# Graph layers of one batch up front instead of two, and each later batch's graph layers four steps ahead of the attention

## What is computed

```
adj = layernorm(x)                        # 256 x 256, used as a soft adjacency
h   = ctx
for W, a_self, a_neigh, b in (layer 0, layer 1):          # two graph attention layers, 8 heads of 32
    feat  = h @ W                                         # per head
    e     = leaky_relu(feat.a_self (rows) + feat.a_neigh (columns), 0.2) - 1e10 * (1 - adj)
    h     = elu(softmax(e) @ feat + b)                    # heads side by side: 256 x 256
x1  = x + h
y   = layernorm(x1)
r   = y + attention(rmsnorm(y))           # 16 query heads, 4 key heads, causal, rotary, q/k rmsnorm
out = x1 + r + mixture(rmsnorm(r))        # 8 experts, the two best of each row, silu(gate) * up, down
```

## Time and profile before

| | |
|---|---|
| median of three runs | 656.95 us |
| profiled execution | 656.72 us, span 654.9 us |
| PE busy | 607.1 us, 93% of the span |
| DVE, POOL, ACT busy | 435.1, 306.8, 269.0 us (66, 47, 41%) |
| mean granted TensorE clock | 0.979 |

### The profile page before, as it was taken

How to read it: one execution, slowest core, us unless ns; L and a number is a source line. 1 busy time by engine, 2 the same in 40 slices (tenths; PEclk the granted TensorE clock), 3 DMA queues, 4 the chain that set the end, 5 groups by cost and what they waited for, 6 DMA issues and landing times.

```text
span 654.9 us, 10357 instructions
## 1 busy us (share of the span) xinstructions
PE 607.1 (93%) x3269; PEld 435.6 (67%) x3269; DVE 435.1 (66%) x1279; ACT 269.0 (41%) x653; POOL 306.8 (47%) x588
## 2 busy tenths in 40 slices
PE   3799899789799999989699999989999998999998
PEld 2278468336677798736587788736668873666886
DVE  4897688598755587599756487466644646664463
ACT  2363454164665342164665342045740204574020
POOL 1493486478844240378854150378630038763000
PEclk9999899889899999999899999989999998999999
DMA  8920000000000000000000000000000000000000
GB/s 285 385 72 3 1 2 1 16 5 2 1 1 2 1 2 17 16 2 1 1 2 1 1 2 0 18 0 2 1 1 1 2 17 1 2 0 2 1 2 16
DMA packets 8729, 14.41 MB, mean 22 GB/s; under 512 B 908, under 2 KB 7372, under 8 KB 8420
## 3 DMA queue, kind: packets, MB, share of 16 engines
q1 hardware_dynamic: 8676, 13.76, 5.9%
HBM read 12.70 MB, written 1.05 MB: 21 GB/s over the span
## 4 chain that ended last, share of the span: by engine, by line
PE 65%; DVE 19%; issue 5%; POOL 5%; ACT 4%; DMA 1%; DVEq 0%; POOLq 0%; SPq 0%; ACTq 0%
PE bank L616 14%; PE bank L514 10%; PE bank L574 5%; PE ob L488 5%; PE bank L638 5%; PE bank L593 4%; PE bank L560 3%; PE tb L477 3%; DVE ssq L1024 2%; PE bank L589 2%; PE bank L585 2%; ACT prob L727 2%; DVE tt L959 2%; DVE m L1021 2%; PE zb L469 2%
## 5 line engine op out<-in xcount | busy, mean ns | idle before, releaser
L560 PE MATMUL bank<-wqkv_sb,hT 128*128 128x512 f32 x192 | 92.8, 623 | 0.8 <-ACT v_sb L703 0.8
L727 ACT ACTIVATE prob<-bank,sneg,rms 128x128 f32<-128x128 f32 (+1 forms) x128 | 64.0, 508 | 58.6 <-DVE sneg L1053 58.4
L837 POOL TENSOR_TENSOR m<-early,rope_s 128x256 f32<-128x256 f32 x80 | 73.1, 938 | 31.4 <-ACT early L708 30.9
L514 PE MATMUL bank<-m,wgu_sb 128*128 128x128 f32 (+1 forms) x480 | 85.6, 329 | 0.7 <-DVE early L1100 0.6
L795 POOL TENSOR_SCALAR tt<-tt,gmn 128x256 f32<-128x256 f32 x96 | 66.9, 706 | 36.2 <-DVE gmn L959 35.8
L514 PEld LDWEIGHTS bank<-m,wgu_sb 128*128 128x128 f32 x480 | 70.9, 191 | 8.9 <-DVE early L1100 2.1
L853 POOL TENSOR_SCALAR prob<-prob,srcp 128x128 f32<-128x128 f32 (+1 forms) x128 | 53.4, 435 | 48.2 <-DVE srcp L1124 48.0
L574 PE MATMUL bank<-kT,qT 128*128 128x128 f32 (+1 forms) x256 | 60.9, 354 | 1.8 <-ACT prob L727 1.8
L616 PE MATMUL bank<-wo_sb,qT 128*128 128x256 f32 x256 | 59.0, 382 | 0.7 <-ACT qT L733 0.7
L560 PEld LDWEIGHTS bank<-wqkv_sb,hT 128*128 128x128 f32 x192 | 35.4, 196 | 36.3 <-issue 33.0
L708 ACT ACTIVATE early<-bank 128x512 f32<-128x512 f32 x40 | 24.1, 602 | 79.5 <-PE bank L560 77.2
(11 more groups left out here) (200 smaller groups left out, 1182.3 us busy)
## 6 DMA issues: line engine op xcount, KB each, us to landing
wqkv_sb<-wqkv_dram SPq DMA_DIRECT2D x1, 3072.0 KB, 12.2
wgu_sb<-wgu_dram SPq DMA_DIRECT2D x2, 1408.0 KB, 10.8
wo_sb<-wo_dram SPq DMA_DIRECT2D x1, 2048.0 KB, 17.6
wd_sb<-wd_dram SPq DMA_DIRECT2D x1, 1408.0 KB, 14.7
out_dram<-rows SPq DMA_DIRECT2D x8, 128.0 KB, 1.7
xin<-x_dram SPq DMA_DIRECT2D x3, 256.0 KB, 2.7
rows<-gat_rows_dram SPq DMA_DIRECT2D x2, 256.0 KB, 2.9
kT<-x_dram SPq DMA_DIRECT2D x1, 256.0 KB, 3.8
```

Source lines behind the costliest of these rows:

```text
L514: mm = pe.matmul(ps[:, m * N + c0:m * N + c1], wgu_sb[:, m, k, n * P:(n + 1) * P], tokT[:, k, c0:c1], start=(k == 0), stop=(k == KT - 1))
L560: mm = pe.matmul(ps[:, :], hT[:, k, t * P:(t + 1) * P], wqkv_sb[:, k, c * G * HD:(c + 1) * G * HD], start=(k == 0), stop=(k == KT - 1))
L727: ins = act.activation(prob[:, n % 5, i * nk:(i + 1) * nk], ps[:, i * nk:(i + 1) * nk], ACT.Exp, bias=sneg[:, n, i:i + 1], scale=rq(g, t, ...
L837: ins = pool.tensor_tensor(dst[:, :, c, :], src[:, :, 1 - c, :], s_, ALU.mult)
```

## The change

`PLAN` has the graph layers of batch 0 alone up front. Those of batch 1 run beside the tail of batch 0, those of 2 beside the tail of 1, those of 3 beside the tail of 2; only the last pass has none. In the passes graph layers and prep stand four steps ahead of the tail: steps 4 to 43 of a pass have the steps 8 to 47 of the next batch's two strands (in the passes after the first the steps 0 to 43 have 4 to 47), and the last four steps have the steps 0 to 3 of the batch after that. Batch 1 has no earlier pass, so the steps 0 to 3 of the first pass have two of its steps each.

With it: one set of buffers, banks and semaphores for the graph layers; two `x1` buffers instead of three; the inputs of batch 1 are loaded behind the weights, those of batch `b + 2` ahead of the stores of batch `b`; the Newton steps of batch 0's layer norm are made by DVE (nine instructions) and not by POOL (twelve); `WAKE` has other places and 127 products; setup work of layer 1 is one step earlier.

```diff
-SET, SEQ, XS = (0, 1, 0, 0), (0, 0, 1, 2), 3
-BEHIND = 2
+SEQ, XS = (0, 1, 2, 3), 2
-TERMS1_AT, ROPE_AT = (15, 16), (25, 26, 27)
-WAKE = {2: 3, 7: 4, 8: 14, 19: 3, 20: 3, 21: 3, 22: 3, 23: 3, 24: 3, 25: 3, 26: 3, 27: 3, 28: 3, 30: 4, 31: 14, 43: 10, 45: 8}
-WAKE.update({s: 2 for s in tuple(range(9, 19)) + tuple(range(32, 43))})
+TERMS1_AT, ROPE_AT = (14, 15), (25, 26, 27)
+WAKE = {1: 2, 2: 4, 5: 2, 6: 2, 7: 2, 8: 14, 18: 5, 20: 3, 22: 3, 24: 6, 28: 3, 29: 3, 30: 3, 31: 12, 41: 18, 43: 6, 45: 3}
+WAKE.update({s: 2 for s in tuple(range(9, 18)) + tuple(range(32, 41))})
+AHEAD = 4
 PLAN = []
 for step in range(STEPS):
-    PLAN += [("gat", 0, step), ("prep", 0, step + PREP_LEAD), ("gat", 1, step - BEHIND)]
+    PLAN += [("gat", 0, step), ("prep", 0, step + PREP_LEAD)]
 for batch in range(B):
     for step in range(STEPS):
-        PLAN += [("gat", batch + 2, step)] if batch + 2 < B else []
-        PLAN += [("prep", batch + 1, step)] if batch + 1 < B else []
+        if batch == 0 and step < AHEAD:
+            PLAN += [("gat", 1, 2 * step), ("gat", 1, 2 * step + 1)]
+        elif batch + 1 < B and step + AHEAD < STEPS:
+            PLAN += [("gat", batch + 1, step + AHEAD), ("prep", batch + 1, step + AHEAD)]
+        elif batch + 2 < B:
+            PLAN += [("gat", batch + 2, step + AHEAD - STEPS)]
         PLAN += [("tail", batch, step)]
...
-            for b in range(2, B):
-                load_inputs(b)
+            load_inputs(1)
             for b in range(B):
+                if b + 2 < B:
+                    load_inputs(b + 2)
                 store(b)
...
-                    if b == 1:
-                        keep_clock(WAKE.get(s + BEHIND, 0))
+                    if b == 0:
+                        keep_clock(WAKE.get(s, 0))
...
(POOL, prep)
-                    for _ in range(3):
-                        newton(link_a, b, ln_y[:, :], ln_a[:, :], ln_v[:, :])
-                    pool.sem_inc(ln_ready, 1)
+                    if b > 0:
+                        for _ in range(3):
+                            newton(link_a, b, ln_y[:, :], ln_a[:, :], ln_v[:, :])
+                        pool.sem_inc(ln_ready, 1)
...
(DVE, prep)
+                    if b == 0:
+                        for _ in range(3):
+                            newton(link_a, b, ln_y[:, :], ln_a[:, :], ln_v[:, :])
+                        dve.sem_inc(ln_ready, 1)
```

More of the change, by code:

```diff
@@ L205, in block_program @@
         wd_sb = sb("wd_sb", [P, JT, D])
[L207 to L215, removed]
+        stats = sb("stats", [P, T, 6])
+        mv = sb("mv", [P, T, 2])
+        rs_v = sb("rs_v", [P, T])
+        rs_y = sb("rs_y", [P, T])
+        rs_a = sb("rs_a", [P, T])
+        gmn = sb("gmn", [P, 3, 2])
+        gsum = sb("gsum", [P, H])
+        sn_res = sb("sn_res", [P, T, 2 * H])
+        parts = sb("parts", [P, T, NP, 2 * H], BF16)
         x1 = [sb(f"x1_{i}", [P, T, D]) for i in range(XS)]
@@ L250, in block_program @@
[L250 to L256, removed]
@@ L261, in block_program @@
+        zs = sb("zs", [P, 2, 2 * N])
+        lr = sb("lr", [P, 2, 2 * N])
+        tt = sb("tt", [P, 3, 2, N])
+        gpT = sb("gpT", [P, 3, 2, T, P])
+        go = sb("go", [P, T, D])
+        gex = sb("gex", [P, T, D])
+        gT = sb("gT", [P, KT, N])
         early = sb("early", [P, 6, G * HD])[:, :, :]
@@ L309, in block_program @@
         hn_ready, ln_seed, pool_a, ln_ready, hid_ready = sem("hn_ready"), sem("ln_seed"), sem("pool_a"), sem("ln_ready"), sem("hid_ready")
[L311 to L321, removed]
+        in_x, in_c, x_used, c_used = sem("in_x"), sem("in_c"), sem("x_used"), sem("c_used")
+        z_full, z_free = sem("z_full"), sem("z_free")
+        t_full, t_free = sem("t_full"), sem("t_free")
+        parts_ready, pair_l_ready = sem("parts_ready"), sem("pair_l_ready")
+        pair_r0_ready, pair_r1_ready = sem("pair_r0_ready"), sem("pair_r1_ready")
+        lrelu_done, score_ready, shifted = sem("lrelu_done"), sem("score_ready"), sem("shifted")
+        pv_done, o_free = sem("pv_done"), sem("o_free")
+        gout_ready, gexp_ready, gres_ready = sem("gout_ready"), sem("gexp_ready"), sem("gres_ready")
         dve_b = sem("dve_b")
@@ L472, in gat @@
+                        pe.wait_ge(z_free, z_value(q, l, k + 1))
+                        pe.matmul(zb[:, :], pair_l[:, t * P:(t + 1) * P],
+                                  pair_r[:, 2 * hp:2 * hp + 2, :].rearrange("k h m -> k (h m)"), start=True, stop=True)\
+                          .then_inc(z_full, 1)
                     for k in units(l, a - TRANS_LAG):
-                        pe.wait_ge(shifted[i], unit(q, l, k) + 1)
-                        pe.wait_ge(t_free[i], t_value(q, l, k + 2))
+                        pe.wait_ge(shifted, unit(q, l, k) + 1)
@@ L687, in gat @@
+                        act.wait_ge(lrelu_done, unit(q, l, k) + 1)
+                        act.activation(zs[:, k % 2, :], zb[:, :], ACT.Copy, scale=-1.0).then_inc(z_free, 1)
                     for k in units(l, a - TRANS_LAG):
-                        act.wait_ge(t_full[i], t_value(q, l, k + 2))
+                        act.wait_ge(t_full, t_value(q, l, k + 2))
                         if k >= 3:
-                            act.wait_ge(pv_done[i], unit(q, l, k) - 2)
-                        act.activation(gpT[i][:, k % 3, :, :, :].rearrange("p h m i -> p (h m i)"), tb[i][:, :], ACT.Exp).then_inc(t_free[i], 1)
+                            act.wait_ge(pv_done, unit(q, l, k) - 2)
@@ new lines, in gat @@
+                            dve.wait_ge(pv_done, unit(q, l, 4 * t + 4))
+                            o_ = ob[:, 0:H * FE].rearrange("p (h o) -> p h o", h=H)
+                            link_a(b, dve.reciprocal(gsum[:, :], o_[:, :, FO]))
+                            g_ = go[:, t, :].rearrange("p (h o) -> p h o", h=H)
+                            dve.tensor_tensor(g_, o_[:, :, 0:FO], gsum[:, :].unsqueeze(2).broadcast_to([P, H, FO]), ALU.mult)\
+                               .then_inc(o_free, 1)
@@ L1228, in _ @@
             link(dve.tensor_copy(identb[:, :], ident))
[L1229 to L1235 removed]
+            for t in range(T):
+                link(dve.memset(feat[:, t, :, FO:FE], 1.0))
+            dve.sem_inc(z_free, 1)
+            dve.sem_inc(t_free, 1)
+            dve.sem_inc(o_free, 1)
+            dve.sem_inc(lrelu_done, 2)
             dve.sem_inc(m1_ready, 3)
```

259 lines of the change are left out of this document (113 added, 146 removed).

## The result

The changed kernel is slower: 670.75 us (median of four runs, 670.39 to 672.04) against 657.11 us for the kernel before on the same chip (four runs, 655.78 to 657.57). The ratio is 1.021, 95% interval 1.019 to 1.024. The forecast was 644. The profiled run took 670.39 us, with a span of 668.6.

A forecast was written before the change was run, and what follows sets the result against it. The prediction took the kernel as one long queue on PE. Its terms, -41.6 + 32.3 + 4 - 7 = -12.3 us on the profiled 656.72, gave 644.4 us, stated as 644, with a range from 632 to 657 us.

The forecast's parts named there:

- A: Stage up front with one batch: first projection at 84.5 us instead of 126.1, a term of -41.6 us.
- walk: One batch followed alone through the stage up front, hand-overs summed in series: first projection at 86.8 us, taken as 84.5.
- B: One more pass with graph layers: +33.7 us, less 1.4 us of batch 1's first products, a term of +32.3 us.
- C: Double graph steps at the start of the first pass: PE waits about 4 us for POOL's shift, +4 us.
- D: Lead of four steps in three passes: long waits go, a shorter one comes; -2.3 us a pass, -7 us together.
- R1: Passes with graph layers: transposes wait behind a Newton run, projections queue behind them; 673 us, chance 0.11.
- R2: Stage up front: PE runs at the low clock, 14 us more, 658 us; chance 0.07.
- sign of D going wrong: Second and third passes: waits for squares, `gpT` and a shift adding up to more than 7 us a pass.
- One of its chances: Whole kernel: chance 0.14 of being slower by more than 2 us.

The follow-up runs named there:

- experiment 6: Changed kernel with only some steps leading by four: second layer's units 654.0 us; second layer, close, prep 663.45; first layer 667.05; both layers' units 667.31.
- experiment 5: Changed kernel with idle products on PE where it waits for POOL's shift (28 in the first pass, 23 in the others): 665.6 us, ratio 1.016.

## Why the prediction was wrong, step by step

**What bounds the kernel.** Right that PE is the queue and that stages add up. The account of the second pass shows what the lead did to it. The changed kernel, cut as in experiment 6:

```profile
243.32:329.39 86.07, 78.62 (x411) 52.43 (x411) 57.31 (x145) 49.24 (x127) 54.06 (x110) 0.94 0.01 4
329.39:363.19 33.80, 32.78 (x201) 26.37 (x200) 21.58 (x80) 9.93 (x17) 10.24 (x18) 1.00 0.00 1
363.19:398.79 35.60, 33.20 (x179) 26.23 (x178) 24.55 (x89) 7.57 (x19) 7.04 (x18) 1.00 0.04 12
```

The kernel without lead:

```profile
230.33:316.35 86.02, 80.19 (x417) 54.71 (x417) 64.12 (x162) 48.86 (x127) 56.26 (x113) 0.94 0.01 4
316.35:344.23 27.88, 27.88 (x154) 21.59 (x153) 17.27 (x65) 10.06 (x18) 9.58 (x16) 1.00 0.00 1
344.23:380.52 36.29, 36.26 (x220) 30.92 (x219) 25.77 (x86) 7.60 (x19) 7.09 (x18) 1.00 0.04 12
```

PE's busy time is 144.60 us with the lead and 144.33 without. Its idle time is 7.45 + 1.02 + 2.40 = 10.87 us with it, and 5.83 + 0.00 + 0.03 = 5.86 without. The difference, 5.0 us, is nearly the whole 5.28 us by which the pass is longer. Without lead PE has no gap at all from the output products to the end of the pass: the graph units fill every wait. The lead took 41 products out of the last stretch, and the gaps opened there.

The lost cover alone doesn't open them, and neither does the close alone. Without lead, DVE has a close among the experts as well (row sum at 346.70 us, ELU at 349.03), and PE doesn't wait: behind the gate it has 56 products of units to do, and with the lead only 8. In experiment 6, with the second layer's units ahead and the close held back, PE also has only 8, and it doesn't wait either (31.03 us of 31.03 busy). So here it takes both.

**A, up front.** Forecast -41.6 us, measured 83.06 - 126.08 = -43.0. Right, though the last microseconds are luck. The walk's parts were near too: DVE's nine Newton instructions took the place of POOL's twelve without a wait, `hn` began at 76.3 and `hT` at 77.8 us. But the 14 idle products took 3.19 us in this trace and not 4.62; in other traces of the same stage they took 4.1 to 4.3, and it lasted 84.9 to 85.3 us. One sum of the walk is 0.9 us short (reckoned as for the second layer, 14.8 + 4 x 1.4 - 0.9 is 19.5, not 18.6), but the 84.5 was set below the walk's 86.8 by judgement and doesn't hang on it.

**B, one more pass.** Forecast 33.7 less 1.4. The passes without lead are 148.9, 150.2 and 149.6 us, and 152.2 for the first pass in the second trace of that kernel, against 148.4 and 148.5 in the earlier trace rows, so the term was about 1.5 us a pass too low. The longest wait is the same 3.9 us; the clock is lower (0.94 in the first stretch of the second pass, 86.02 us, against 0.98 in the same stretch before, 84.60 us). Behind that wait it is 0.50 for 9.5 us here, and before it was 0.63 for 4.6 us (315.54 to 320.14). Why it is, no run tells.

**C, the double steps.** Forecast 4 us. The wait is 6.7 us, and the first pass is 160.26 - 155.47 = 4.8 us longer than the second. Right in kind, 0.8 us low by this measure; but without lead the first pass is 1.3 us shorter than the second in one trace and 2.0 us longer in the other, so the term is known to some 3 us only.

**D, the lead. This step failed, by its sign.** The prediction had: "So the wait of 2.3 or 3.9 us behind that run should go", and "the transposes of unit 1 must now wait for a shift behind the keys' Newton run, about 2 us, in place of 1.5 us for the keys themselves", with "Net of what goes and comes -3 us a pass", taken as -2.3. The second pass became 5.3 us longer than without lead, which is 7.6 us off. The third became 2.8 us longer, though it lacks the first products of a further batch, which take 1.8 us in the second pass (389.13 to 389.68 and 392.67 to 393.95): about 7 us off. The three passes together are 10.3 + 9.5 + 8.4 = 28.1 us over the forecast's 150, 146 and 144; A gave 1.4 us back, and that makes the miss of 26.75 us. B has about 4.5 us of it, and D, with what C fell short, some 23. Three things went into D, as the second pass shows them:

- The wait for the shift is 5.4 us, not 2. PE was done with its other work at 255.0 us; the Newton run ended 2.5 us later, and the unit's shift (two instructions) then took 2.58 us, against 1.25 in the earlier trace rows. Behind it the clock was low for 7.5 us (260.38 to 267.87). All this cost about as much as the removed waits had: the first stretch is as long with lead as without (86.07 and 86.02 us), though it has 1.6 us less work. Net +1.6 us, where -2.3 was expected. The low clock is not new: without lead it stands behind the wait of 3.9 us, here from that wait's end on:

```profile
271.02:280.48 9.46, 9.46 (x37) 7.73 (x38) 7.42 (x18) 4.67 (x11) 7.43 (x18) 0.50 0.00 0
```

- The middle stretch has a wait of 1.02 us for DVE's `go`, which beside the experts was covered.
- In the experts' stretch DVE has the row sum, the ELU and `x1` in front of the experts' own products, and PE waits 2.4 us. PE's longer wait there and DVE's timeline:

```profile
374.29 1.99 PE L500 MATMUL bank<-m,wgu_sb 128*128 128x256 f32 x8 [2.04 <-DVE early L1088]
```

```profile
365.18 0.21 DVE L950 RECIPROCAL gsum<-ob 128x8 f32<-128x8 f32 x1 [0.29 <-PE ob L474]
...
367.02 0.42 DVE L1088 SCALAR_TENSOR_TENSOR early<-pT,bank 128x256 f32<-128x256 f32 x1
367.48 0.29 DVE L959 TENSOR_SCALAR gex<-gex 128x256 f32<-128x256 f32 x1
...
368.83 0.43 DVE L970 BATCH_NORM_STATS2 x_stats<-x 128x6 f32<-128x256 f32 x1
369.30 0.42 DVE L1084 SCALAR_TENSOR_TENSOR pT<-pT,bank 128x256 f32<-128x256 f32 x1
...
375.40 0.17 DVE L879 TENSOR_SCALAR ln_y<-ln_a 128x4 int32<-128x4 int32 x1
375.72 0.42 DVE L1084 SCALAR_TENSOR_TENSOR pT<-pT,bank 128x256 f32<-128x256 f32 x1
```

Between 365.2 and 377.7 us DVE is busy for 11.05 of 12.50 us (without lead, at the same distance behind the gate, for 9.95). The prediction read from "107 of 148 us" that DVE had room; that was an average over the pass. It looked for what the lead does only where the two long waits were, and asked nowhere what the moved units had covered until then. "`hT` four steps early changes nothing" fell with it: the steps that lead up to `hT` (moments and first guess, 374.52 to 375.57 us) stand on DVE in just that stretch.

**The rivals.** R1 (673 us) came nearest, and its mechanism is there: the wait for the shift and the lowered clock in all three passes. But it priced them as a pure addition, with 3 us for the low clock that no row shows, and they largely replaced the old waits; that its total is near is in part the second loss, which it did not name. Up front nothing showed of R2: the clock of that stage is 0.98 (0.96 before), and the 14 idle products took less time than before. The low clock came in another place, behind the 5.4 us wait, where four projections took 3.76 us instead of 1.98. The Trainium skill says in "TensorE: Matmul & The Clock Gate", Part 1, that the slow clock is the default and that activity lifts it; the trace agrees (0.51 behind the wait, 1.00 from 268 us on). The prediction's own sign of D going wrong, more than 7 us of waits for a shift in a pass, did not come: they are 6.7, 5.4 and 5.4 us. The sign left out the waits for DVE, with which they are 8 to 10 us. One of its chances is also a little low: R1 and two thirds of R2 are 0.16, not 0.14.

**What stays open.** The first layer's lead costs some 13 us by the table. By passes, the trace of that kernel is 9.4, 6.3 and 0.3 us above the kernel without lead (6.1, 6.2 and 0.3 above its second trace), though the wait for the shift stands in all three, with 5.4 us or more. The third lacks the first products of a further batch, so that the lead costs it some 2 us; three times that is about half of the loss at most. The first pass has the double steps, 4.8 us in the account. The second loses time mostly in its last stretch, at a clock of 0.92, which the changed kernel doesn't show in that pass and no run explains. So the table's losses don't add up place by place, and how the 5 us of a pass divide between a first and a second layer is not settled. Nor is the price of the low clock by itself.

## What to carry to other kernels

Work that runs beside a main strand is also the cover for that strand's waits: before moving it, list the waits that it hides where it stands, not only those that it may remove where it goes, and list on each engine what it will stand in front of there. Read the load of an engine from the stretch that the work moves into, since an engine at 70% of a pass can be nearly full for the 12 us that count. And try the parts of a change alone: here one half was worth 0.5 to 0.8%, and the other cost 2.6 to 3.0%.

## What the runs showed of the hardware

- One wait of PE of 5.4 us, in a stretch that is otherwise dense, was followed by 7.5 us at a granted clock of 0.51 (four projections 3.76 against 1.98 us, eight small products 1.75 against 0.98). A wait of 3.9 us was followed by 9.5 us at 0.50 in the kernel without lead, and by 4.6 us at 0.63 in the kernel before; what makes the difference was not tested.
- The shift of one unit on POOL, two instructions of one shape, took 1.25 us at 249.59 and 2.58 us at 257.75, and the keys' Newton run 5.2 us here against 4.4 in the earlier trace rows. DVE was at work beside them; what stretched them was not tested.
- With one batch, the stage up front lasted from 79.6 to 85.3 us in the traces of these kernels (86.4 in that of experiment 5, at the lower clock). Two things sort them. With batch 1's first products in it, which the lead of the first layer puts there, it took 83.1 and 83.4 us where the 14 idle products took 3.19 us, and 84.9 to 85.3 where they took 4.1 to 4.3; without them it took 79.6 and 79.8 us (3.19 and 3.20), or 81.2 to 81.4 (3.95 to 4.15). So the same code differs by some 2 us from one execution to the next, with the time of its first idle products, and a difference of 2 us in this stage of one trace is no evidence by itself.
